# Two layers of graph attention on one core: 32x32 blocks turned by VectorE and exchanged through DRAM take the place of TensorE's transposes, with every engine's order rewritten

## The reference

```
layer(h):   u = h h^T / sqrt(384);  a = softmax(u);  delta = a * adj
            attn = delta / (sum(delta) + 1e-10)
            ctx = (attn above the diagonal) (h Wl^T + bl) + diag(attn) (h Ws^T + bs)
                  + (attn below the diagonal) (h Wr^T + br)
            out = relu((ctx - mean) / sqrt(var + 1e-12) * g + beta)
result = layernorm(x + layer2(layer1(x)), eps 1e-5)
```

## Time and profile before

| | |
|---|---|
| median of 3 runs | 1699.22 us |
| the profiled execution | 1699.16 us |
| its span, first to last instruction | 1697.4 us |
| mean granted TensorE clock | 0.994 |
| PE busy | 98% of the span |
| DVE busy | 84% |
| POOL busy | 67% |
| ACT busy | 52% |
| DMA engines busy | 18.5% of 16 engines |

### The profile page before, as it was taken

One profiled execution on the slowest core, in us unless ns is written; L12 is line 12 of the kernel. 1 busy time (PEld: TensorE's weight loads), 2 busy tenths in 40 slices (PEclk: granted clock), 3 DMA queues, 4 the chain that ended last, 5 costly groups with the idle time before them and its releaser, 6 DMA issues.

```text
span 1697.4 us, 34570 instructions
## 1 busy us (share of the span) xinstructions
PE 1670.7 (98%) x10112; PEld 1652.4 (97%) x10112; DVE 1429.1 (84%) x4496; ACT 882.3 (52%) x2182; POOL 1131.2 (67%) x1798
## 2 busy tenths in 40 slices
PE   7999999999999999999999999999999999999996
PEld 7999999999999999999999999999999999999995
DVE  6888888888888888888888888888888888888887
ACT  4555545554555555455545554555555455545553
POOL 2666676666666666766666666667676666666663
PEclk9999999999999999999999999999999999999998
DMA  4112111111111121111111111111121111111111
GB/s 166 49 52 62 51 57 53 59 53 55 59 54 57 51 61 51 57 52 61 51 57 58 55 57 51 59 54 57 51 62 51 57 57 56 56 52 57 56 46 39
DMA packets 93905, 97.63 MB, mean 58 GB/s; under 512 B 10688, under 2 KB 92864, under 8 KB 93888
## 3 DMA queue, kind: packets, MB, share of 16 engines
q1 hardware_dynamic: 93888, 97.43, 18.5%
HBM read 72.22 MB, written 25.17 MB: 57 GB/s over the span
## 4 chain that ended last, share of the span: by engine, by line
PE 97%; DVE 1%; ACT 0%; issue 0%; DMA 0%; POOL 0%; SPq 0%; DVEq 0%; POOLq 0%; ACTq 0%
PE p_proj L305 71%; PE p_gather L363 16%; PE p_score L299 5%; PE p_gather L385 2%; PE p_attnT L344 2%; PE p_score L337 1%; DMA w_raw<-WT 0%; DVE p_gather L437 0%; DVE proj L462 0%; DVE w L496 0%; DVE stats L406 0%; DVE y L443 0%; ACT w L607 0%; ACT proj_split L587 0%; POOL rstd L671 0%
## 5 line engine op out<-in xcount | busy, mean ns | idle before, releaser
L305 PE MATMUL p_proj<-w,hT_layer 128*128 128x384 f32 x6912 | 1406.6, 344 | 0.2 <-DVE w L496 0.2
L305 PEld LDWEIGHTS p_proj<-w,hT_layer 128*128 128x128 f32 x6912 | 1153.7, 189 | 9.5 <-DVE w L496 0.7
L667 POOL TENSOR_TENSOR attnT_split<-attnT,attnT_split 128x256 fp32r<-128x256 f32 x256 | 189.4, 740 | 449.2 <-DVE rows L481 442.4
L215 POOL TENSOR_TENSOR proj_split<-proj,proj_split 128x768 fp32r<-128x768 f32 x252 | 465.2, 1846 | 5.3 <-issue 5.3
L591 ACT ACTIVATE normed<-gathered,nbias,rstd 128x384 f32<-128x384 f32 x128 | 90.7, 709 | 443.7 <-POOL nbias L675 443.7
L363 PE MATMUL p_gather<-proj_split,attnT_split 128*128 128x384 f32 x1536 | 310.9, 337 | 7.8 <-DVE y L443 4.3
L363 PEld LDWEIGHTS p_gather<-proj_split,attnT_split 128*128 128x128 f32 x1536 | 271.9, 189 | 8.4 <-issue 6.1
L462 DVE TENSOR_TENSOR proj<-p_proj,bias_all 128x768 f32<-128x768 f32 x256 | 243.6, 951 | 6.0 <-PE p_proj L305 5.9
L671 POOL TENSOR_TENSOR rstd<-veps,neg_half 128x1 f32<-128x1 f32 x384 | 210.6, 548 | 49.9 <-DVE neg_mean L420 27.9
L582 ACT ACTIVATE attnT_split<-attnT 128x256 fp32r<-128x256 f32 x256 | 105.0, 410 | 243.5 <-DVE attnT L488 243.5
L299 PE MATMUL p_score<-hT_layer 128*128 128x256 f32 x768 | 215.6, 283 | 5.0 <-POOL hT_layer L707 5.0
(11 more groups left out here) (48 smaller groups left out, 1679.3 us busy)
## 6 DMA issues: line engine op xcount, KB each, us to landing
xt_raw<-xT SPq DMA_DIRECT2D x128, 192.0 KB, 2.4
xn<-x SPq DMA_DIRECT2D x128, 192.0 KB, 2.4
out<-o SPq DMA_DIRECT2D x128, 192.0 KB, 1.9
adj_layer<-adj SPq DMA_DIRECT2D x256, 64.0 KB, 1.9
w_raw<-WT SPq DMA_DIRECT2D x6, 576.0 KB, 7.4
bias_all<-bias SPq DMA_DIRECT2D x2, 576.0 KB, 9.0
gain<-gain_row SPq DMA_DIRECT2D x1, 192.0 KB, 9.6
shift<-shift_row SPq DMA_DIRECT2D x1, 192.0 KB, 9.9
```

What stands on the lines that cost most here:

```text
L215: op.tensor_tensor(proj_split[k][:, LO], proj[k][:, UP:LOW + 1, :], proj_split[k][:, HI].bitcast(F32), ALU.subtract).then_inc(s_proj_lo[k], 1)
L305: return nc.tensor.matmul(p_proj[:, which, 0:D], hT[k][:, slot, st, c, :], w[:, k, which, mv, c, :], start=(n == 0), stop=(n == 8))
L667: nc.gpsimd.tensor_tensor(AT_split[k][:, LO], AT[k][:], AT_split[k][:, HI].bitcast(F32), ALU.subtract).then_inc(s_side_lo[k], 1)
```

## The change

What it does:

- The attention matrix is no longer transposed on TensorE. `mask` now ends with a DVE `transpose`, which turns each 32x32 block of `A` in place within the grid (`A_blocks`), and takes the diagonal there from `A` and an identity that lies in PSUM (`ident_p`). SP stores `A_blocks` to DRAM (`store_attn`) and loads it back with rows and columns of blocks exchanged (`load_attn`): four DMAs, each to 32 partitions, with runs of 32 elements (128 bytes). `cut_sides` then runs on POOL from SBUF.
- The normalised rows of layer 1 go the same way: `block_rows` on DVE (128x384), `store_rows`, and `load_rows`: four DMAs of 32 partitions with 12 runs of 128 bytes each. ACT's gain, shift and relu read `rowsT` in SBUF and write the PSUM tile `relu_T`, which has moved to the bank `p_rows`.
- The last graph (`direct`) keeps TensorE's transposes.
- On TensorE the scores of layer 2 stand at n = 4, 6, 8 and its `cross` at n = 16 in PA; in PC the scores of layer 1 stand at n = 0, 2, 4 and `cross` at n = 8 (it was 14 in both).
- The order of DVE, ACT, POOL and SP in an iteration is rewritten. `output_rows` works on graph `i-4` near the start of DVE's iteration (it was `i-3`, at its end).

The core of the diff (declarations, the last graph's branches and the removed lines of the orders are cut):

```diff
# SP
+            def store_attn(k, b, slot):
+                done(sp, s_attn_blocks[k], b)
+                sp.dma_start(attn_mem[k][slot], A_blocks[k][:]).then_inc(s_attn_out[k][slot], 16)
+            def load_attn(k, b, slot):
+                moved_and_done(sp, s_attn_out[k], b, slot, s_side[k])
+                blocks = attn_mem[k][slot].rearrange("(r a) (s b) -> s a r b", a=B, b=B)
+                for s in range(4):
+                    sp.dma_start(AT_whole[k][s * B:(s + 1) * B, :].rearrange("a (r b) -> a r b", b=B),
+                                 blocks[s]).then_inc(s_attn_in[k][slot], 16)
+            def store_rows(b, slot):
+                done(sp, s_rows_blocks, b)
+                sp.dma_start(rows_mem[slot], rows_blocks[:]).then_inc(s_rows_out[slot], 16)
+            def load_rows(b, slot):
+                moved_and_done(sp, s_rows_out, b, slot, s_relu)
+                blocks = rows_mem[slot].rearrange("(r a) (c s b) -> s a c r b", a=B, b=B, c=C)
+                for s in range(4):
+                    sp.dma_start(rowsT[s * B:(s + 1) * B, :, :].rearrange("a c (r b) -> a c r b", b=B),
+                                 blocks[s]).then_inc(s_rows_in[slot], 16)
# TensorE
-            def project_and_score(i, k, b, slot, other, b_other, slot_other, b_before, b_gather=None):
+            def project_and_score(i, k, b, slot, other, b_other, slot_other, b_before, first, last_part,
+                                  b_gather=None):
-                    if score and n == 14:
+                    if score and n == last_part:
                         done(pe, s_cross[other], b_other)
-                    done(pe, s_attn[k], b)
-                    nc.tensor.transpose(p_attnT, A[k][:], ident[:]).then_inc(s_attnT[k], 1)
+                    done(pe, s_self_biased[before], b_last)
-                project_and_score(i, 0, i, p, 1, i - 2, p, i - 3)
+                project_and_score(i, 0, i, p, 1, i - 2, p, i - 3, 4, 16)
-                project_and_score(i, 1, i - 2, p, 0, i + 1, q, i)
+                project_and_score(i, 1, i - 2, p, 0, i + 1, q, i, 0, 8)
# VectorE
+                    nc.vector.transpose(A_blocks[k][:], A[k][:]).then_inc(s_attn_blocks[k], 1)
+                nc.vector.tensor_tensor_reduce(diag_scratch[k][:], A[k][:], ident_p[k], 1.0, 0.0, ALU.mult,
+                                               ALU.add, col(rows[k], slot, DIAG)).then_inc(s_diag[k], 1)
+            def block_rows(b):
+                done(dve, s_normed, b)
+                nc.vector.transpose(rows_blocks[:], normed[:]).then_inc(s_rows_blocks, 1)
# GpSimd
+            def cut_sides(k, b, slot):
+                gathered_in(pool, s_attn_in[k], b, slot)
+                nc.gpsimd.tensor_tensor(AT[k][:], AT_whole[k][:].unsqueeze(1).broadcast_to([P, 2, N]), sides[:],
+                                        ALU.mult).then_inc(s_side[k], 1)
```

More of the change, by code:

```diff
@@ L272, in iteration @@
                     sp.dma_start(xt_raw[:, q], xT[i + 3]).then_inc(s_xt[q], 16)
+                if live(i, i - 1) and not direct(i, i - 1):
+                    store_rows(i - 1, q)
+                if live(i, i - 2) and not direct(i, i - 2):
+                    store_attn(1, i - 2, p)
+                if live(i, i - 1) and not direct(i, i - 1):
+                    load_rows(i - 1, q)
                 if live(i, i):
@@ L280, in iteration @@
                     sp.dma_start(xn[:, p], x[i - 2]).then_inc(s_xn[p], 16)
+                if live(i, i - 2) and not direct(i, i - 2):
+                    load_attn(1, i - 2, p)
                 if live(i, i + 3):
@@ L326, in project_and_score @@
                         last = project_step(k, slot, UP + n // 9, n % 9)
[L327 to L329 removed]
+                    if score and n == first:
+                        done(pe, s_lo[other], b_other)
+                        done(pe, s_diag[other], b_other - 1)
+                    if score and n >= first and (n - first) % 2 == 0 and (n - first) // 2 < C:
+                        step = score_step(other, slot_other, (n - first) // 2)
+                        if (n - first) // 2 == C - 1:
                             step.then_inc(s_parts[other], 1)
@@ L518, in iteration @@
                     normalise_layer1(i, q)
+                if live(i, i - 4):
+                    output_rows(i, p)
+                if last_graph(i):
+                    add_bias(1, i - 2, True)
+                if live(i, i - 2):
+                    done(dve, s_score[1], i - 2)
+                if live(i, i - 1) and not direct(i, i - 1):
+                    block_rows(i - 1)
+                if live(i, i - 2):
+                    scaled_scores(1, i - 2, p)
                 if live(i, i):
@@ L592, in normalise, with relu_rows @@
                                      scale=rstd[:, which:which + 1]).then_inc(s_rows, 1)
+            def relu_rows(i, b, slot):
+                if isinstance(i, int) and i == 1:
+                    act.wait_ge(s_const, 64)
+                done(act, s_lo[1], b - 1)
+                if direct(i, b):
+                    done(act, s_normedT, 0)
+                    rows_in = relu_T
+                else:
+                    gathered_in(act, s_rows_in, b, slot)
+                    rows_in = rowsT[:]
+                for c in range(C):
+                    last = nc.scalar.activation(relu_T[:, c, :], rows_in[:, c, :], ACT.Relu,
+                                                bias=shift1[:, c:c + 1], scale=gain1[:, c:c + 1])
+                last.then_inc(s_relu, 1)
+                done(act, s_relu, b)
+                done(act, s_self[1], b - 2)
+                nc.scalar.activation(hT[1][:, slot, HI], relu_T, ACT.Copy).then_inc(s_hi[1], 1)
             def finish(i, p):
@@ L750, in iteration @@
                     done(pool, s_attn[0], i + 1)
-                if live(i, i - 2) and not last_graph(i):
-                    low_sides(1, i - 2)
+                if live(i, i - 2):
+                    if direct(i, i - 2):
+                        low_sides(1, i - 2)
+                    else:
+                        cut_sides(1, i - 2, p)
                 if live(i, i + 1):
```

175 lines of the change are left out of this document (103 added, 72 removed).

## The result

The changed kernel takes 2198.85 us (median of 4 runs, 2195.57 to 2199.78) against 1699.32 us: 1.294 of the time before, 95% interval 1.291 to 1.296. I had forecast 1725 and a range of 1655 to 1795. The direction was right and the size wrong by a factor of about twenty, and the mechanism that I had put first is not the one that sets the time.

What follows compares the result with a forecast made beforehand. PE bounded the kernel at 12.97 us a period; after the change loop A would, at 13.10. 124 iterations add 16 us and fill 10 to a span of 1697.4: forecast 1725 us, own range 1708 to 1750, wide range 1655 to 1795.

Steps and rivals of the forecast that it cites:

- PE's saving: On PE, two attention and three row transposes leave each iteration: 0.55 us, period 12.42 us, 70 us if nothing else binds.
- Loop A: Through DVE, POOL, ACT, PE: ACT's finish waits for POOL's late deviation_output, ahead of cross_scores; 13.10 us per period, sets the pace.
- Loop B: Layer 1's rows through DRAM, from block_rows back to low_rows on DVE: 12.6 us at 15 ns a packet, 13.7 at 26.
- rival B: Loop B sets the pace because 128-byte packets are dear: at 26 ns 101 us more, 1800 us; chance 23%.
- signs that I had set for a wrong mechanism: PE waiting at s_lo or at a gather, or rowsT landing over 4.3 us after its first load is issued.
- The store lands 1.9 us after its issue: Rows' store on SP: block_rows done at 4.5 us from DVE's first operation, store landed at 6.45.
- The exchange itself: Rows' trip through DRAM: store landing in 1.9 us, four loads 0.36 us apart; 5.2 us to ACT's first relu.
- Small packets: DMA cost of a 128-byte packet in the exchanges: between 10 and 26 ns, taken as 15.
- Nearly slack-free: Attention's loads land at about 12 us; POOL has until 14 for 2 us of work; if late, costs less than loop B.
- Fill: Start of the kernel, first exchanges with no work over them: 10 us more, 5 and 20 as ends.
- rival C: An exchange much dearer than the rows say, kernel about 1970 us at 40 ns, or PE's clock falling when idle; chance 6%.
- the 47%: Chance given to the forecast itself, 1725 us with own range 1708 to 1750; slower in all had 76%.

Runs made afterwards that it cites:

- kernel 4: Changed kernel with both exchanges through DRAM left out and ACT's finish moved behind the exponentials: 1660.41 us, 0.977 of the kernel before the change.
- kernel 3: Changed kernel with both exchanges through DRAM left out, data read where the block transposes put them: 1739.79 us, 1.025 of the kernel before the change.
- kernels 1 and 7: First: changed kernel with xT's load last on SP, 1833.76 us. Second: the same, but rowsT loaded as whole 1536-byte rows, 1760.69 us.
- kernel 10: Changed kernel, xT last on SP, finish behind exponentials, rowsT loads split SP/ACT, plus output statistics behind add_bias and store_attn(1) behind load_rows: 1764.50 us.
- kernel 8: Changed kernel with xT's load last on SP and ACT's finish behind the exponentials, both exchanges kept: 1838.25 us, 1.081 of the kernel before the change.

## Why the prediction was wrong

- *PE's saving.* Right in its price, not in full in what it gave. With the row transposes kept the period is 12.77 against 12.75 forecast. With all of them gone (kernel 4) it is 12.6 against 12.42, so the most seen is 0.35 us a period and 39 us of the kernel, not 0.55 and 70: about 0.15 of the rest is PE's wait for `low_input` at the first score matmul of PC, which the forecast did not have.
- *Loop A.* Forecast 13.10 us, measured 13.26 in kernel 3, with the mechanism and all its stations; kernel 4 shows it by opening it. But in the changed kernel it is covered and costs nothing.
- *Loop B.* The loop of rival B is closed, but at 16.77 us, not 12.6 to 13.7, and not for rival B's reason, dear packets. The signs that I had set for a wrong mechanism are there: PE waits 2.3 us a period at `s_lo` for layer 2's input, and the last `rowsT` lands 4.6 us after the first load is issued (1116.42 to 1121.01), over my 4.3. The step that failed is the one that says "The store lands 1.9 us after its issue": it lets the store be issued as soon as `block_rows` is done. I had checked the attention's store in front of the loads, but passed over the load of `xT(i+3)` in front of the store, though it waits for `low_input`, which my own loop A puts at 6.2 us. SP's longest wait is this one, 3.8 us (1109.50 to 1113.34), not the one for the stored attention that the prediction names. By my own numbers the store could not go before 6.2 + 0.4 = 6.6; the trace has 1113.75 - 1106.99 = 6.76 from DVE's first operation, against 4.5. The sum was available without any unknown cost; I costed SP by its issue time and not by what each of its waits holds back.
- *The exchange itself.* From the store's issue to ACT's first relu 5.2 us forecast, 7.28 measured (1113.75 to 1121.03): 0.6 because `xT`'s data is ahead of the store, 0.9 because the loads of 384 runs are issued 0.65 us apart and not 0.36, 0.6 from the last issue to relu, 2.7 instead of 2.1. The rest of the loop, 2.7, was forecast at 2.9. So of 4.2 us missing, 2.26 are the queue order and 2.08 the exchange, less 0.17.
- *Small packets.* 15 ns as the mean of the mix, about 13 for one of 128 bytes, against 15 taken and 26 feared. The rule of the Trainium skill ("DMA: Bandwidth & Descriptors", Specifications) that small transfers below 512 B fall off line rate points the right way. In these runs the price shows in the issue of the loads and in their landing (0.64 against 0.44 us and 2.4 against 1.9, kernels 1 and 7), not as 26 ns a packet.
- *The attention's exchange and POOL.* "Nearly slack-free", as I wrote: it costs 13 us alone, and becomes the bound in kernel 10. But I put its cost at less than loop B's, with the data landing at about 12 us. Behind the late store and loads of the rows, `cut_sides(1)` starts 16.5 us after DVE's first operation, and the way through it closes most periods of the changed kernel.
- *Fill.* I took 10 us. 3.80 x 124 = 471 us of the 499 are the steady state, 28 are left for fill and drain (24 with the mean period of 16.81), over my end of 20. I did not take them apart.
- *The clock* (part of rival C). PE waits 2.3 us a period at `s_lo`, and the granted clock falls (us, busy (x) of PE, PEld, DVE, ACT and POOL, clock, DMA share, GB/s):

```profile
1104.00:1106.60 2.60, 0.32 (x2) 0.00 (x0) 0.55 (x2) 2.30 (x5) 0.00 (x0) 0.96 0.45 104
1106.60:1108.00 1.40, 1.34 (x5) 1.34 (x6) 1.36 (x4) 0.98 (x3) 1.21 (x4) 0.50 0.67 221
```

From 1106.6 us it is 0.5, the level of 1.2 GHz. PE was busy 0.32 of the 2.6 us before. PE is in neither way in which the period closes, so the slower clock should cost nothing on top; the mean clock is 0.934 instead of 0.994.
- *Chances.* 76% on slower was right, but the 47% stood on loop A, which the exchange covers; the direction came true by another mechanism than the one that I had put first. The range was too narrow because its upper end came from one dearer packet, while the loop that mattered had several terms without a row (issue of many runs, landing behind other data) and a station that I had left out.

## What to carry to other kernels

On an in-order queue the cost of a DMA can be its wait (365 us here) rather than its issue: for each new store or load on a path that closes within an iteration, list every instruction in front of it on that queue and when the semaphore of each one comes. A round trip of 192 KB through DRAM, back in short runs, took 7.3 us here and more than 6 without any wait in front of it; it seems to need a consumer a whole iteration away, not the next free place, which I did not try. And when several loops close at nearly the same length, removing work from the longest engine can gain nothing until each is opened (kernel 8 against kernel 4), so write them all down with their sums before sizing any of them.

## What the hardware showed that I had not expected

- An issue on SP takes longer for a load of very many runs: 0.64 us for 384 runs of 128 bytes, 0.44 for the same bytes in 32 rows of 1536 (1.77 for four). It is not proportional: 128 runs of 128 bytes also took 0.44 (L309, 1.75 for four), and 128 rows of 1536 bytes 0.33.
- A 192 KB store lands in 1.9 us, and in 2.7 when a 192 KB load was issued on the same queue 0.4 us before.
- DVE's block transpose of fp32 takes 0.31 us for 128x128 and 0.57 for 128x384, close to other operations of that length (0.29 and 0.56).
